# Filter stage of a Mamba, attention and spectral-filter block: the lower left quarter of the block Toeplitz product with three products in place of four

## The chip, the cores and the metric

One core of one Trainium2 chip runs the whole program. The metric is device time in microseconds from one launch; lower is better. TensorE does the matrix products, VectorE (DVE) and ScalarE (ACT) the elementwise work, GpSimd (POOL) a share of it, and SyncE (SP) issues the DMAs. All data is float32. The matmuls of this stage read their operands as pairs of a rounded part ("high", in a float32r tile) and a rest ("low").

## The reference, cut to what matters

The program computes a two-way Mamba block with group norm, then causal attention, then a mixture of four spectral filter experts, on 4 batches of 1024 tokens with 64 channels. The change touches only the last part and the preparation of its filters:

```python
def _stu_conv(phi, u, n):            # phi (L, 16), u (b, sl, 64)
    Vf = rfft(phi, n=n, axis=0)
    Uf_p = rfft(u, n=n, axis=1); Uf_m = rfft(u * sgn3, n=n, axis=1)
    U_plus  = irfft(Vf[None, :, :, None] * Uf_p[:, :, None, :], n=n, axis=1)[:, :sl]
    U_minus = irfft(Vf[None, :, :, None] * Uf_m[:, :, None, :], n=n, axis=1)[:, :sl] * sgn
    return U_plus, U_minus
out = einsum('btkd,k,kde->bte', U_plus, s, Mpp) + einsum('btkd,k,kde->bte', U_minus, s, Mpm)
# x = t + stu mixture (experts see the first 1/1, 1/2, 1/4, 1/8 of the tokens) + 3 taps of u
```

In the time domain each of the 16 filters is a causal convolution of 1024 tokens, that is, a product with a lower triangular Toeplitz matrix. Even and odd tokens are held apart, so each filter gives two sources (even, odd) and two lags.

## The kernel before, in words

The program has three stages with a barrier between them: the Mamba stage, the attention stage and the filter stage (`expert_stage`), which begins 667 us into the profile.

In the filter stage the batches are taken in two pairs (`q`), the 64 channels of both batches of a pair side by side on 128 rows. For each pair there are 16 filters, so 32 filters in all. A filter has two steps, `source` 0 and 1. A step is one call of `convolve`: for a Toeplitz product of 512 half-rate tokens in blocks of 128, it multiplies token blocks (stationary operand, `u_high` or `u_low`) with shifted windows of the filter (`hankel`, moving operand), two lags at a time. The out bank of 512 columns for the first half of the tokens needs block offsets 0 and 1, the one for the second half offsets 0 to 3. Each offset takes three matmuls (`TERMS`: high by high, low by high, high by low): 18 matmuls a step, of which 12 have 512 columns and 6 have 256.

TensorE's order for a filter is: step 0, then `mix` of the filter before (10 matmuls with `block_mix`), then step 1. The first filter of each pair of batches is followed by `taps_and_residual`. ScalarE copies each half out of PSUM into a float32r tile (L1973), one copy for each batch of the pair, 64 rows each; VectorE subtracts that copy from the PSUM value and writes the low part (L2010). Each source has its own PSUM tile `ps_conv` of two banks, so TensorE waits only for the low parts of two steps before. SyncE loads the filter windows of filter m (`load_hankel`, L1607) once filter m-2 is done, into one of two slots. GpSimd forms `block_mix` for the coming filter (L1733, L1737).

The filters' rows are made in the attention stage: GpSimd reverses and splits `phi` (`filter_rows`, L1637 and L1638), SyncE stores them in DRAM (L1618) and loads the first two windows; GpSimd goes on with `weigh_and_sum`, `even_matrices` (L1697, which overwrites the memory in which `phi` lay) and then `rstd2`, a step of the attention chain (L1055).

The work of each engine is written out by hand in program order; counting semaphores tie the engines together.

Of the kernel before, what the change touches and what calls it, by code (L numbers as in the profile page):

```python
# [26 lines left out]
B = 4  # L27
# [20 lines left out]
PADS = 640  # L48
BLOCKS = 2
# [53 lines left out]
def norm_tensors(nc, ctx):  # L103
# [6 lines left out]
    g.mixed = sb("mixed", [C, L])  # L110
# [27 lines left out]
def load_sums(sp, g, b):  # L138
# [69 lines left out]
def mamba_stage(nc, ins, a, g, e, x1):  # L208
# [4 lines left out]


    with ExitStack() as ctx:
# [105 lines left out]
        with nc.Block() as block:  # L321

            @block.sync
            def _(sp):
# [52 lines left out]
                def unit(u, i):  # L377
                    sp.wait_ge(bc_out, 16 * (u + 1))
                    for s in range(N):
# [6 lines left out]
                        if i == 0 and u:  # L386
                            if s == 9:
                                store_sums(sp, g, u // 2 - 1)
                            if s == 11:
                                load_sums(sp, g, u // 2 - 1)  # L390
# [579 lines left out]
def attention_stage(nc, ins, a, g, e, x1, x2, u_all, u_high, u_low):  # L970

    with ExitStack() as ctx:
# [66 lines left out]
        with nc.Block() as block:  # L1039

            @block.sync
            def _(sp):
                store_sums(sp, g, B - 1)
                load_sums(sp, g, B - 1)
# [3 lines left out]
            def _(pool):  # L1048
# [24 lines left out]
                weigh_and_sum(nc, pool, e, EXPERTS + 2, 2 * EXPERTS)  # L1073
                even_matrices(nc, pool, e)
# [486 lines left out]
def weight_tensors(nc, ctx):  # L1561

    def sb(name, shape, dt=F32):
# [10 lines left out]
        ar_step ar_ready block_step block_ready passed phi_in plus_in minus_in"""  # L1574
    (e.logits_in, e.weights_in, e.w_step, e.softmax_ready, e.wk_ready, e.sum_step, e.rows_step, e.rows_ready,
     e.filters_out, e.ar_step, e.ar_ready, e.block_step, e.block_ready, e.passed, e.phi_in, e.plus_in,
     e.minus_in,
# [5 lines left out]
def expert_tensors(nc, ctx, e):  # L1583
# [19 lines left out]
    e.filters = nc.dram_tensor("filters", (FILTERS, 4, PADS), F32, kind="Internal").ap()  # L1603


def load_hankel(sp, e, k, slot):
    sp.dma_start(e.hankel[slot][:, :, 0:H + 1].bitcast(F32),  # L1607
                 bass.AP(e.filters.tensor, k * 4 * PADS, [[1, 128], [PADS, 4], [1, H + 1]])
                 ).then_inc(e.hankel_in[slot], 16)


def load_expert_weights(sp, ins, e):
# [8 lines left out]
    for slot in range(2):  # L1621
        load_hankel(sp, e, slot, slot)

# [7 lines left out]
def filter_rows(nc, pool, e):  # L1631
# [3 lines left out]
    for lag in range(2):  # L1635
# [3 lines left out]
            e.rows[:, 2 * lag + 1, 0:H], reverse, e.rows[:, 2 * lag, 0:H].bitcast(F32), ALU.subtract))  # L1639

# [51 lines left out]
def even_matrices(nc, pool, e):  # L1692

    pool.wait_ge(e.filters_out, 16)
# [45 lines left out]
def expert_stage(nc, ins, att, e, x2, u_all, u_high, u_low, out):  # L1740
# [11 lines left out]
    with ExitStack() as ctx:  # L1752
# [12 lines left out]
        shifted = sb("shifted", [C, BANKS, H])  # L1765
# [6 lines left out]
        ps_conv = [ctx.enter_context(nc.psum_tensor(f"ps_conv{i}", [128, 2, 2, H // 2], F32)) for i in range(2)]  # L1772
# [7 lines left out]
        names = """pads_ready ut_psum ut_high ut_low conv_half conv_psum conv_high conv_low mixed_in shift_ready  # L1780
            out_done"""
        (pads_ready, ut_psum, ut_high, ut_low, conv_half, conv_psum, conv_high, conv_low, mixed_in, shift_ready,
# [10 lines left out]
        with nc.Block() as block:  # L1793

            @block.sync
            def _(sp):
                for q in range(PAIRS):
                    with sp.Fori(1 - q, FILTERS // 2) as pair:
                        for slot in range(2):
                            k = 2 * pair + slot  # L1800
                            sp.wait_ge(conv_psum, STEPS * (q * FILTERS + k - 1))
                            load_hankel(sp, e, k, slot)
                for q in range(PAIRS):
# [22 lines left out]
            def _(pe):  # L1826
# [7 lines left out]
                def convolve(slot, q, source):  # L1834

                    shift = source
                    hankel = e.hankel[slot]
# [241 lines left out]
```

## Time and profile before

| what | value |
| --- | --- |
| median of 3 runs | 981.84 us (980.28 to 983.69) |
| the profiled execution's own time | 984.49 us |
| its span, first to last instruction | 982.6 us |
| busy over the span | PE 86%, PEld 50%, DVE 74%, ACT 52%, POOL 54% |
| mean granted TensorE clock | 0.939 of full speed |

PE stands for matmuls, PEld for the loads of the stationary operand. In a timeline row the first number is the start in microseconds from the span's start, the second the time covered, "x2" means that two instructions are merged in the row, and the bracket at the end tells how long the engine sat idle before it and what ended that. All durations that the prediction uses come from this one execution.

### The profile page before, as it was taken

To read this page: it belongs to the slowest core of one execution; us is meant where nothing else is said; L and a number is where in the kernel's file an instruction comes from. 1 tells how busy PE (TensorE), PEld (TensorE's weight loads), DVE (VectorE), ACT (ScalarE), POOL (GpSimd) and SP (SyncE) were. 2 spreads that over 40 slices of the span, in tenths; PEclk is the share of its full clock that TensorE was granted. 3 is DMA by queue.
4 is the path that set the end of the run, shared out by engine and by line. 5 is a ranking of instruction groups with operands and counts; after the bars stand their busy time and mean duration, and the time that the engine had idled before them with its cause. 6 is when DMAs were issued, how large, how long until landed. Compare 5 with 4: busy or idle time off the path is not lost. (4 is left out here: it accounts for less than half of the span.)

```text
span 982.6 us, 10220 instructions
## 1 busy us (share of the span) xinstructions
PE 841.4 (86%) x3004; PEld 493.4 (50%) x3004; DVE 722.8 (74%) x774; ACT 511.6 (52%) x706; POOL 534.3 (54%) x366
## 2 busy tenths in 40 slices
PE   5768798887989788886586998958999999999996
PEld 1223233332333233332234554527888888888885
DVE  1999989989999999999965446634666566565664
ACT  4635656555566556644305366545455555454553
POOL 4577878879888897876625965311222221122220
PEclk9779989899999999997977899988999999999998
DMA  7778897878979898787609900001243344233432
GB/s 174 275 241 336 300 311 254 324 265 277 334 235 371 276 322 286 299 308 233 219 0 103 180 1 1 1 0 44 87 128 114 100 128 128 87 99 115 128 108 63
DMA packets 75348, 178.23 MB, mean 181 GB/s; under 512 B 24514, under 2 KB 25044, under 8 KB 75300
## 3 DMA queue, kind: packets, MB, share of 16 engines
q1 hardware_dynamic: 75316, 177.85, 56.8%
q8 instruction: 14, 0.23, 0.1%
q14 instruction: 18, 0.15, 0.0%
HBM read 175.57 MB, written 2.26 MB: 181 GB/s over the span
## 5 line engine op out<-in xcount | busy, mean ns | idle before, releaser
L451 POOL TENSOR_TENSOR prod<-hidden,c_wide 128x1024 f32<-128x1024 f32 x128 | 300.8, 2356 | 99.0 <-DVE hidden L882 93.4
L546 PE MATMUL ps_y<-prod,ident 128*128 128x512 f32 x512 | 247.3, 627 | 42.8 <-POOL prod L451 42.7
L882 DVE TENSOR_TENSOR_SCAN hidden<-decay,ps_d 128x1024 f32<-128x1024 f32 x99 | 226.0, 2283 | 9.9
L1850 PE MATMUL ps_conv<-hankel,u_high 128*128 128x512 f32 (+1 forms) x768 | 215.5, 362 | 0.0
L546 PEld LDWEIGHTS ps_y<-prod,ident 128*128 128x128 f32 x512 | 98.2, 198 | 185.7 <-issue 117.1
L1850 PEld LDWEIGHTS ps_conv<-hankel,u_high 128*128 128x128 f32 x768 | 138.7, 189 | 25.4 <-issue 0.3
L2010 DVE TENSOR_TENSOR stack<-ps_conv,stack 64x512 fp32r<-64x512 f32 x128 | 88.3, 690 | 68.8 <-ACT stack L1973 66.4
L1850 PE MATMUL ps_conv<-hankel,u_low 128*128 128x512 f32 (+1 forms) x384 | 138.1, 360 | 0.0
L1733 POOL CAST block_mix<-even 128x256 fp32r (+1 forms) x32 | 12.7, 398 | 218.9 <-PE ps_tail L1832 218.9
L868 DVE TENSOR_TENSOR ps_d<-ps_x,b_wide 128x1024 f32<-128x1024 f32 x99 | 122.0, 1232 | 4.5
L2010 DVE TENSOR_TENSOR qk<-ps_conv,qk 64x512 fp32r<-64x512 f32 x128 | 88.3, 690 | 50.0 <-ACT qk L1973 47.2
L1973 ACT ACTIVATE stack<-ps_conv 64x512 fp32r<-64x512 f32 x128 | 76.0, 594 | 82.3 <-PE ps_conv L1850 80.4
L1973 ACT ACTIVATE qk<-ps_conv 64x512 fp32r<-64x512 f32 x128 | 76.0, 594 | 62.3 <-PE ps_conv L1850 60.3
L732 ACT ACTIVATE decay<-dt_b,a_neg_b 128x1024 f32<-128x1024 f32 x51 | 58.0, 1144 | 70.8 <-DVE hidden L882 70.4
L1850 PEld LDWEIGHTS ps_conv<-hankel,u_low 128*128 128x128 f32 x384 | 72.9, 190 | 13.8
L732 ACT ACTIVATE decay<-dt_f,a_neg_f 128x1024 f32<-128x1024 f32 x48 | 54.2, 1142 | 38.4 <-DVE hidden L882 37.1
L441 POOL TENSOR_TENSOR drive<-dtx,b_wide 128x1024 f32<-128x1024 f32 x29 | 68.4, 2358 | 6.7 <-ACT dtx L727 6.7
L1460 DVE TENSOR_REDUCE max_parts<-ps_s 128x1 f32<-128x512 f32 (+1 forms) x48 | 27.5, 598 | 27.1 <-PE ps_s L1144 13.4
L882 DVE TENSOR_TENSOR_SCAN hidden<-ps_d,drive 128x1024 f32<-128x1024 f32 x14 | 32.1, 2290 | 9.3 <-ACT ps_d L738 5.4
L1055 POOL TENSOR_TENSOR small<-small,minus_half 128x8 f32<-128x8 f32 x4 | 6.6, 1645 | 57.3 <-DVE small L1430 57.3
L1324 ACT ACTIVATE probs<-ps_t 128x512 f32<-128x512 f32 (+1 forms) x48 | 24.8, 521 | 23.0 <-PE ps_o L1186 22.8
L882 DVE TENSOR_TENSOR_SCAN hidden<-ps_w,drive 128x1024 f32<-128x1024 f32 x15 | 34.2, 2279 | 0.0
(306 smaller groups left out, 1187.7 us busy)
## 6 DMA issues: line engine op xcount, KB each, us to landing
b_wide<-bc_rows SPq DMA_DIRECT2D x128, 512.0 KB, 5.5
c_wide<-bc_rows SPq DMA_DIRECT2D x128, 512.0 KB, 5.4
hankel<-filters SPq DMA_DIRECT2D x32, 1026.0 KB, 5.2
plus<-in_M_phi_plus SPq DMA_DIRECT2D x2, 1024.0 KB, 13.2
minus<-in_M_phi_minus SPq DMA_DIRECT2D x2, 1024.0 KB, 18.8
x_pair<-in_x SPq DMA_DIRECT2D x2, 768.0 KB, 8.6
bc_rows<-dt_low SPq DMA_DIRECT2D x8, 128.0 KB, 4.9
out<-plus SPq DMA_DIRECT2D x4, 256.0 KB, 4.9
```

Source lines behind the costliest of these rows:

```text
L441: nc.gpsimd.tensor_tensor(drive[:, :], dtx[:, :], b_wide[s % BC_DEEP][:, :], ALU.mult).then_inc(share_ready, 1)
L451: nc.gpsimd.tensor_tensor(prod[k % PAIR][:, :], hidden[k % DEEP][:, :], c_wide[s % BC_DEEP][:, :], ALU.mult).then_inc(prod_ready, 1)
L546: mm = nc.tensor.matmul(out, ident[:, :], halves(prod[k % PAIR])[h], start=False, stop=(k % N == N - 1))
L732: nc.scalar.activation(decay[decay_slot(s, last)][:, :], dt[i][:, :], ACT.Exp, scale=a_neg[i][:, s:s + 1]).then_inc(decay_ready, 1)
L868: nc.vector.tensor_tensor(ps_d[:, :], ps_x[:, :], b_wide[s % BC_DEEP][:, :], ALU.mult).then_inc(drive_ready, 1)
L882: nc.vector.tensor_tensor_scan(hidden[k % DEEP][:, order], left[:, order], right[:, order], 0.0, ALU.mult, ALU.add).then_inc(hidden_ready, 1)
L1324: nc.scalar.activation(probs[n % 2][:, 0:hi - lo], ps_t[n % 2][:, 0:hi - lo], ACT.Exp).then_inc(probs_ready, 1)
L1460: nc.vector.tensor_reduce(max_parts[:, i, at // H:at // H + 1], ps_s[c % 2][:, 0:n], AX.X, ALU.max, negate=True).then_inc(part_ready, 1)
L1733: nc.gpsimd.tensor_copy(dst[:, :, 0, :], src).then_inc(e.block_step, 1)
L1850: mm = nc.tensor.matmul(out, pairs[q][wp][:, 2 * delta + source, :], rows, start=(delta == 0 and term == 0), stop=(delta == 2 * half + 1 a ...
L1973: nc.scalar.activation(stacks[slot][0:C, source, b, :, half * 2 * HEAD:(half + 1) * 2 * HEAD], ps_conv[source][lanes(b), half, :, :], ACT. ...
L2010: nc.vector.tensor_tensor(low, ps_conv[source][lanes(b), half, :, :], high.bitcast(F32), ALU.subtract).then_inc(conv_low, 1)
```

## The change

The second half of the out tokens takes from the first half of the in tokens a 2 by 2 block of Toeplitz blocks (offsets 1, 2, 2 and 3 in units of 128). Its four block products are replaced by three: one of the filter windows at offset 2 with the difference of the two token blocks (`gap`), which both outputs share with opposite sign, and one for each output with the sum of two filter windows (`hankel_sums`). The shared product lands in a PSUM tile of its own (`ps_common`, both sources in one bank), ScalarE keeps it as two copies with signs +1 and -1 in SBUF (`common`), and VectorE adds it to the late half (`late`). The late half's high and low parts are then made from that SBUF tile. The early half has one PSUM bank for both sources (`ps_early`), where before each source had its own.

The sums of filter rows are made by GpSimd between `weigh_and_sum` and `even_matrices`, stored by SyncE, and loaded with each filter beside the windows. `gap` and its two parts are made by VectorE as the stage's first work. Some tiles move: `shifted` lies in the memory of `x1`, `gap_parts` in `k_low`, `common` and `late` in attention tiles.

```diff
+def load_sums(sp, e, hankel_sums, k, slot):
+    sp.dma_start(hankel_sums[slot][:, :, 0:SUM_ROW - 1].bitcast(F32),
+                 bass.AP(e.filter_sums.tensor, k * 4 * SUM_TAPS, [[1, 128], [SUM_TAPS, 4], [1, SUM_ROW - 1]])
+                 ).then_inc(e.hankel_in[slot], 16)
...
+def filter_sums(nc, pool, e):            # called between weigh_and_sum and even_matrices
+    pool.wait_ge(e.filters_out, 16)
+    for lag in range(2):
+        reverse = e.phi[:, lag::2][:, ::-1]
+        chain_on(pool, e.sums_ready, 3 * lag + 1, nc.gpsimd.tensor_tensor(
+            e.pair_sum, reverse[:, 128:128 + SUM_TAPS], reverse[:, 0:SUM_TAPS], ALU.add))
+        chain_on(pool, e.sums_ready, 3 * lag + 2, nc.gpsimd.tensor_copy(e.sum_rows[:, 2 * lag, :], e.pair_sum))
+        chain_on(pool, e.sums_ready, 3 * lag + 3, nc.gpsimd.tensor_tensor(
+            e.sum_rows[:, 2 * lag + 1, :], e.pair_sum, e.sum_rows[:, 2 * lag, :].bitcast(F32), ALU.subtract))
...
 def even_matrices(nc, pool, e):
-    pool.wait_ge(e.filters_out, 16)
+    pool.wait_ge(e.sums_out, 16)
...
 # SyncE: at the end of load_expert_weights
+    sp.wait_ge(e.sums_ready, 6)
+    sp.dma_start(e.filter_sums..., e.sum_rows...).then_inc(e.sums_out, 16)
 # SyncE: filter stage
+                for slot in range(2):
+                    load_sums(sp, e, hankel_sums, slot, slot)
...
                             load_hankel(sp, e, k, slot)
+                            load_sums(sp, e, hankel_sums, k, slot)
 # TensorE (terms issues the three matmuls of TERMS with n columns for each lag)
-                    for half in range(2):
-                        for delta in range(2 * half + 2):
...
+                    at_least(pe, common_kept, 2 * t)
+                    terms(ps_common[source], gaps[q], source, hankel, row, H - 1 - 2 * HEAD, HEAD, source,
+                          first=True, last=True).then_inc(common_psum, 1)
+                    at_least(pe, early_low, 2 * t)
+                    terms(ps_early, data, source, hankel, row, H - 1, 2 * HEAD, source, first=True)
+                    terms(ps_early[:, :, HEAD:], data, 2 + source, hankel, row, H - 1, HEAD, source,
+                          last=True).then_inc(conv_early, 1)
+                    at_least(pe, late_ready, t - 1)
+                    terms(late_out, data, 4 + source, hankel, row, H - 1, 2 * HEAD, source, first=True)
+                    terms(late_out[:, :, HEAD:], data, 6 + source, hankel, row, H - 1, HEAD, source)
+                    terms(late_out[:, :, 0:HEAD], data, 2 + source, sums, SUM_ROW, 2 * HEAD - 1, HEAD, source)
+                    terms(late_out[:, :, HEAD:], data, source, sums, SUM_ROW, HEAD - 1, HEAD, source,
+                          last=True).then_inc(conv_psum, 1)
...
-                    pe.wait_ge(e.hankel_in[slot], 16 * (q * FILTERS // 2 + pair + 1))
-                    at_least(pe, conv_low, PIECES * (t - 1))
+                    pe.wait_ge(e.hankel_in[slot], 32 * (q * FILTERS // 2 + pair + 1))
+                    if first and q == 0:
+                        pe.wait_ge(gap_ready, 3)
 # ScalarE, each step
-                        for half in range(2):
-                            act.wait_ge((conv_half, conv_psum)[half], t + 1)
-                            for b in range(2):
-                                nc.scalar.activation(stacks[slot][0:C, source, b, :, half * 2 * HEAD:(half + 1) * 2 * HEAD],
-                                                     ps_conv[source][lanes(b), half, :, :], ACT.Copy).then_inc(conv_high, 1)
+                        act.wait_ge(common_psum, t + 1)
+                        at_least(act, late_ready, t - 1)
+                        for block, sign in enumerate((1.0, -1.0)):
+                            nc.scalar.activation(common[source][:, :, block, :], ps_common[source], ACT.Copy,
+                                                 scale=sign).then_inc(common_kept, 1)
+                        act.wait_ge(conv_early, t + 1)
+                        for b in range(2):
+                            nc.scalar.activation(stacks[slot][0:C, source, b, :, 0:2 * HEAD], ps_early[lanes(b), :, :],
+                                                 ACT.Copy).then_inc(early_high, 1)
+                        act.wait_ge(late_ready, t + 1)
+                        for b in range(2):
+                            nc.scalar.activation(stacks[slot][0:C, source, b, :, 2 * HEAD:],
+                                                 late[source][lanes(b), :, :, :].rearrange("p l k i -> p l (k i)"),
+                                                 ACT.Copy).then_inc(late_high, 1)
 # VectorE, each step (before: four subtractions from ps_conv, each after its copy)
+                        for b in range(2):
+                            dve.wait_ge(early_high, 2 * t + b + 1)
+                            nc.vector.tensor_tensor(low, ps_early[lanes(b), :, :], high.bitcast(F32),
+                                                    ALU.subtract).then_inc(early_low, 1)
+                        dve.wait_ge(conv_psum, t + 1)
+                        dve.wait_ge(common_kept, 2 * t + 2)
+                        at_least(dve, late_low, 2 * (t - 1))
+                        nc.vector.tensor_tensor(late[source]..., ps_late[source],
+                                                common[source]..., ALU.add).then_inc(late_ready, 1)
+                        for b in range(2):
+                            dve.wait_ge(late_high, 2 * t + b + 1)
+                            nc.vector.tensor_tensor(low, late[source][lanes(b), :, :, :]...,
+                                                    high.bitcast(F32), ALU.subtract).then_inc(late_low, 1)
 # VectorE, start of the stage: gap = difference of token blocks, its high part, its low part
```

## Rows read from the trace of the kernel before

**Rows 1.** Chain that ended last, two filters: start, time covered, engine, tile, line.
```profile
851.25 7.13 PE ps_conv L1850 x36
858.38 0.48 PE ps_low L1832 x4
858.86 0.47 PE ps_mid L1832 x2
...
860.25 7.12 PE ps_conv L1850 x36
```

**Rows 2.** Busy time by stretch: us, then PE, PEld, DVE, ACT, POOL, clock, DMA share, GB/s.
```profile
851.25:860.25 9.00, 9.00 (x47) 7.60 (x47) 5.52 (x9) 4.75 (x8) 2.17 (x4) 1.00 0.37 118
...
560.00:600.00 40.00, 36.64 (x174) 21.14 (x173) 24.45 (x65) 20.37 (x45) 26.62 (x13) 1.00 0.11 38
...
973.70:976.50 2.80, 2.67 (x10) 1.73 (x10) 1.34 (x4) 1.68 (x4) 0.00 (x0) 0.76 0.00 0
```

**Rows 3.** Groups of instructions from 600 us on, by form: busy us, mean ns, idle before.
```profile
L1850 PE MATMUL ps_conv<-hankel,u_high 128*128 128x512 f32 x512 | 184.2, 400 | 0.0
...
L2010 DVE TENSOR_TENSOR stack<-ps_conv,stack 64x512 fp32r<-64x512 f32 x128 | 88.3, 690 | 68.8 <-ACT stack L1973 66.4
L1973 ACT ACTIVATE stack<-ps_conv 64x512 fp32r<-64x512 f32 x128 | 76.0, 594 | 82.3 <-PE ps_conv L1850 80.4
```

**Rows 4.** Timeline of one step's half on ScalarE and VectorE.
```profile
800.14 1.21 ACT L1973 ACTIVATE stack<-ps_conv 64x512 fp32r<-64x512 f32 x2 [1.73 <-PE ps_conv L1850]
800.76 1.41 DVE L2010 TENSOR_TENSOR stack<-ps_conv,stack 64x512 fp32r<-64x512 f32 x2 [1.53 <-ACT stack L1973]
```

**Rows 5.** Timeline of ScalarE in the attention stage: copies from PSUM and from SBUF.
```profile
568.59 0.39 ACT L1324 ACTIVATE probs<-ps_t 128x256 f32<-128x256 f32 x1
568.87 1.06 ACT L1295 ACTIVATE xn_t<-ps_p 64x512 f32<-64x512 f32 x2
...
654.32 0.63 ACT L1289 ACTIVATE u_high<-u_all 128x512 fp32r<-128x512 f32 x1
654.86 0.37 ACT L1324 ACTIVATE probs<-ps_t 128x256 f32<-128x256 f32 x1
```

**Rows 6.** Timeline of the start of the filter stage.
```profile
667.56 1.08 PE L1909 MATMUL ps_low<-ident,u_all 128*128 128x128 f32 x4 [9.30 <-PEq L1039]
670.85 0.70 PE L1850 MATMUL ps_conv<-hankel,u_high 128*128 128x512 f32 x1
678.30 0.33 PE L1832 MATMUL ps_low<-u_t,ar_mix 128*128 128x128 f32 x2
685.51 0.50 PE L1850 MATMUL ps_conv<-hankel,u_high 128*128 128x512 f32 x1
675.92 4.29 DVE L2010 TENSOR_TENSOR qk<-ps_conv,qk 64x512 fp32r<-64x512 f32 x6
```

**Rows 7.** Landing of L1607's loads, of L1618's store; packets in one 9 us stretch.
```profile
DMA to landing us min/median/max: 5.1/5.2/8.3
...
DMA to landing us min/median/max: 3.6/3.6/3.6
...
DMA packets 528, 1.05 MB, mean 117 GB/s; under 512 B 16, under 2 KB 16, under 8 KB 528
```

**Rows 8.** Timeline: last mix of the program; then where the first pair's result is taken.
```profile
973.78 0.74 PE L1832 MATMUL ps_low<-stack,block_mix 128*128 128x256 f32 x4 [2.13 <-DVE stack L2010]
...
827.43 1.27 DVE L2016 TENSOR_TENSOR plus<-ps_tail,shifted 64x512 f32<-64x512 f32 x2
829.40 0.34 PE L1832 MATMUL ps_low<-u_t,ar_mix 128*128 128x128 f32 x2
```

**Rows 9.** GpSimd: `filter_rows`, then `even_matrices` and what follows it.
```profile
L1638 POOL TENSOR_TENSOR even<-even x2: 1348/1348/1348, 529.6 to 531.8; 16x512 fp32r<-16x512 f32 x2
...
572.30 9.68 POOL L1697 TENSOR_TENSOR even<-plus,minus 128x1024 f32<-128x1024 f32 x4 [0.17 <-POOL minus L1685]
594.55 1.65 POOL L1055 TENSOR_TENSOR small<-small,minus_half 128x8 f32<-128x8 f32 x1 [12.57 <-DVE small L1430]
```

More of the change, by code:

```diff
@@ L48 @@
 PADS = 640
+SUM_TAPS = 384
+SUM_ROW = 258
 BLOCKS = 2
@@ L208, in mamba_stage @@
 def mamba_stage(nc, ins, a, g, e, x1):
+    a.x1, a.both = x1, g.both
     with ExitStack() as ctx:
@@ L1832, in add_out @@
                     return nc.tensor.matmul(dst, w_block, data, start=first, stop=True, skip_group_check=True)
-                def convolve(slot, q, source):
-                    shift = source
-                    hankel = e.hankel[slot]
-                    row = H + 2
-                    for half in range(2):
-                        for delta in range(2 * half + 2):
-                            first = 128 * delta
-                            lo = max(first, half * 2 * HEAD)
-                            n = (half + 1) * 2 * HEAD - lo
-                            out = ps_conv[source][:, half, :, 2 * HEAD - n:]
-                            for term, (wp, dp) in enumerate(TERMS):
-                                rows = bass.AP(hankel, dp * row + H - 1 + first - lo,
-                                               [[4 * row, 128], [2 * row + shift, 2], [-1, n]])
-                                mm = nc.tensor.matmul(out, pairs[q][wp][:, 2 * delta + source, :], rows,
-                                                      start=(delta == 0 and term == 0),
-                                                      stop=(delta == 2 * half + 1 and term == len(TERMS) - 1))
-                        mm.then_inc((conv_half, conv_psum)[half], 1)
@@ new lines, in _, with terms @@
+                gaps = [[part[:, :, 2 * q:2 * q + 2, :].rearrange("p s b c -> p s (b c)") for part in gap_parts]
+                        for q in range(PAIRS)]
+                def terms(out, data, tile, rows, pitch, at, n, shift, first=False, last=False):
+                    for term, (wp, dp) in enumerate(TERMS):
+                        mm = nc.tensor.matmul(out, data[wp][:, tile, :],
+                                              bass.AP(rows, dp * pitch + at, [[4 * pitch, 128], [2 * pitch + shift, 2], [-1, n]]),
+                                              start=first and term == 0, stop=last and term == len(TERMS) - 1)
+                    return mm
@@ new lines, in convolve @@
+                def convolve(slot, q, source, t):
+                    hankel, sums, data = e.hankel[slot], hankel_sums[slot], pairs[q]
+                    row = H + 2
+                    late_out = ps_late[source]
+                    at_least(pe, common_kept, 2 * t)
[11 more added lines that the diff above has]
+                          last=True).then_inc(conv_psum, 1)
```

62 lines of the change are left out of this document (41 added, 21 removed).

## Prediction

> **What bounds the kernel now.** I read the chain of waits first. In the filter stage it is TensorE and nothing else [rows 1]: 36 convolution matmuls in 7.12 us, 10 mix matmuls in 1.87 us (858.38 to 860.25), 9.0 us for a filter, with no wait between. The busy times of the same 9 us say the same: PE 9.00, VectorE 5.52, ScalarE 4.75 [rows 2]. The groups by form show where the slack lies: the copies L1973 waited 82 us for TensorE and the subtractions L2010 69 us for the copies [rows 3]. So a shorter TensorE program pays here for as long as ScalarE and VectorE keep up, and the question is what their new order does.
>
> **TensorE's work.** The mean of a matmul (400 ns for 512 columns, [rows 3]) is latency, since they overlap. Spacing counts: ps_mid has 2 of 512 columns in 0.47 us, 0.235 each; ps_low has 4 of 256 in 0.48, 0.12 each [rows 1]. Check: 24 x 0.235 + 12 x 0.12 = 7.08, against 7.12 measured. Before, a step has 12 and 6. After, it has 6 of 512 (early 3, late 3) and 15 of 256 (common 3, early 3, late 9): 3 more instructions, but 768 columns fewer. For a filter that is 12 x 0.235 + 30 x 0.12 = 6.4 us, 0.7 less. With the mix, 8.27 in place of 9.0. The other bound, that a matmul of 256 columns costs more in runs of 9 than in runs of 4, is not borne out by [rows 1]; at 0.13 it would cost 0.3 a filter.
>
> **The new loop between ScalarE and VectorE.** Before, a step's four copies and four subtractions ran behind TensorE with no way back in a step. Now a step t has, on ScalarE in this order: two copies of the common product, C; two early copies, E; then a wait for VectorE's addition; two late copies, L. On VectorE: two early subtractions, the addition, two late subtractions. Both are strictly in order. So L(t) is followed by C(t+1) and E(t+1); the last E(t+1) releases the second early subtraction; behind that stands the addition of t+1; and it releases L(t+1). This ring closes once a step, without TensorE in it. Nothing in it overlaps but the first subtraction with the second E. Its length, from the start of E:
> - first E to first subtraction: 800.14 to 800.76, 0.62 [rows 4]
> - two subtractions 1.41 [rows 4]; the second starts after 0.71, later than the second E ends plus hand-over, so it adds nothing
> - addition, 128x512 with one operand in PSUM: the trace has no such form; the subtraction with one operand in PSUM takes 0.69 [rows 3], plus 0.03 ahead of it (1.41 less two times 0.69) and 0.03 hand-over (0.62 less 0.594): 0.75
> - two L, source in SBUF: the nearest row is 0.63 [rows 5], not the 0.594 of PSUM. In the pair of [rows 4] the second starts 0.02 after the first ends (1.21 less 2 x 0.594), so 2 x 0.65 = 1.30. Other pairs overlap: u_high takes 0.63 but the next starts after 0.54, and the xn_t pair takes 1.06 for two of 0.58 [rows 5]. The two L read different halves of the rows, like the pair L1973; I take 1.30, lower bound 1.08
> - two C, 128x256 from PSUM: 0.38 by itself, the next starting 0.28 later (568.59 to 568.87) [rows 5]. They read the same rows, so I take 0.28 each, 0.56; upper bound 2 x 0.40 = 0.80
>
> Sum 0.62 + 1.41 + 0.75 + 1.30 + 0.56 = 4.64 us a step, bounds 4.42 and 4.88. A filter is two: 9.28, bounds 8.84 and 9.76. TensorE needs 8.27 and must now wait, 1.0 us a filter, where it starts the early product and needs the early bank free (`early_low`; one bank where each source had its own). Against 9.0 now (8.98 over the stage) this is +0.30 a filter, bounds -0.14 and +0.78.
>
> ScalarE's busy time is 0.56 + 1.21 + 1.30 = 3.1 a step, VectorE's five times 0.69 with gaps 3.55: neither is full. It is the order that binds. Break-even is a ring of 4.49 a step; under 4.13 TensorE binds again.
>
> On ScalarE the trace shows both: the pair L1973 does not overlap, the xn_t pair does, by 0.1 us. The Trainium skill ("ScalarE: Activation LUTs", section "What ACT_TABLE_LOAD costs") states that back-to-back ACTIVATEs overlap by about 93 ns, without exception. By that rule the L pair would be 1.11 and E 1.09. The ring would be some 0.2 shorter, which is rival A; the 1.21 of L1973 speaks against the rule for pairs that change rows, and the sum goes by that row.
>
> **Filters outside the steady state.** By following the same durations through: the two filters after each taps block find ScalarE and VectorE caught up (the block is 7.2 us of TensorE alone, 678.30 to 685.51, [rows 6]) and run at TensorE's pace, -0.7 each. That is three in all, -2.1, since of the second pair's two one is used up: there ScalarE's four `shift` copies now stand behind L, so VectorE's fold ends about 2.2 us after the convolution, where before it ended 0.7 ahead of the taps (828.70 against 829.40) [rows 8]; +2.2 less the 0.7 is +1.5. The remaining 27 filters at +0.30: +8.1.
>
> **Start of the stage.** TensorE began its first convolution at 670.85 [rows 6]. It now waits for 32 on the load semaphore, so for the first sums, issued when the stage begins (about 667.9). A load of 1,026 KB takes 5.2 us to landing, up to 8.3 for the two issued together [rows 7]; of it 3.3 are transfer (DMA share 0.37 of 9 us, [rows 2]). Half the bytes in as many packets: 3.5 if bytes count, 5.2 if packets count, 8.3 at worst. I take 4.8: landed at 672.5, 1.7 late. Then step 0 (3.2) and common 0.36 end at 676.1, but the early product of step 1 waits for the early subtractions of step 0. VectorE is busy with `u_t` until 675.9 [rows 6], then does them to 677.4. So both steps end at 677.5 + 1.07 + 1.78 = 680.35, against 678.30 [rows 6]: **+2.05** (bounds +1 and +5.5). The three `gap` instructions on VectorE (3 x 0.69) end at 669.7, when `u_t` was waiting for ScalarE anyway: nothing.
>
> **Tail.** The last mix waited 2.13 us for the low parts [rows 8]. Now the addition (0.75) stands ahead, and L is 0.04 slower: +0.8.
>
> **What lies beside other work.** The GpSimd sums: 6 instructions of 16x384, from 1.35 us for 16x512 [rows 9] at most 6 us with waits, then SyncE's store (the like store took 3.6, [rows 7]): `even_matrices` is about 9.6 us later. It ended at 582.0 and GpSimd then waited 12.6 us for VectorE [rows 9], so 3 us of cover are left; were it 10 us longer, 7 would fall on the attention chain. Filter loads: windows plus sums take 7.5 (by bytes) to 9.2 us (by packets) from the release, with a second issue on SyncE; the time until they are needed is one filter, 9.3, plus the 1.0 of TensorE's wait. Hidden, but nearly used up. The windows' slots and `mixed_in` are as before.
>
> **Sum.** +8.1 -2.1 +1.5 +2.05 +0.8 = +10.3. For the unseen waits (each addition now has three) I add up to 1 us in all: **+11** on the profiled execution's 984.49. The median shown is 2.65 less, 981.84; the forecast is 993.
>
> **Rivals.**
> A. All copies overlap by 0.1 us. For it: most pairs in the attention stage do [rows 5]. Against: the 256 copies of L1973 do not. Ring 4.40, a filter 8.8, 27 x -0.18 = -4.9, with the other terms -3: 979. By the Trainium skill's rule above this is the case.
> B. The other side: the ring does not bind and TensorE does. This needs a ring under 4.13, for instance if the sequencers let L or the addition start on data ready earlier, or VectorE's forms with both rows full were faster than 0.69. Then 31 x -0.72 = -22, start and tail +3: 962. Decides below 4.49 a step. Against it: each link is a row, and their sum would have to be 0.5 off.
> C. The ring is longer: C without overlap (0.80), hand-overs double, or DMA or GpSimd slows VectorE. Ring 4.88, 27 x 0.78 = 21, plus 2.3: 1005.
> D. TensorE's waits of 1 us lower its clock. In the attention stage it was idle 8% of the time at a clock of 1.00 [rows 2]; after the 2.1 us idle of the tail it was 0.76 over 2.8 us [rows 2, 8]. If it were at 1.2 GHz for a tenth of the stage, 30 us of work would cost 26 more, of which the waits hide 3: 1015.
>
> **How the numbers follow.** Forecast 0.58, A 0.17, B 0.08, C 0.14, D 0.03. What can be told from no change here is about 0.3%, 3 us. Faster: B and half of A, 0.16. Same: the other half, and a little of the forecast's low end: 0.10. Slower: 0.74. The forecast's own range is 987 to 999; the range of 8 in 10 is 978 to 1007.
>
> **What would show it.** In the steady stretch, a filter of 9.3 us with TensorE 8.3 busy; the idle time ahead of the first early matmul, ended by VectorE's early subtraction, about 1 us once a filter; ScalarE's L released by the addition with no slack, and the addition starting 0.03 after the second subtraction. Clock 1.00. If TensorE waits on the load semaphore instead, the load budget was wrong; if it waits nowhere, B holds. If `rstd2` at 594.55 moves, the cover on GpSimd was not there.

## The result, and the profile after

| | before | after |
|---|---|---|
| median (range), us | 981.09 (980.28 to 983.69), 4 runs | 996.58 (993.78 to 1001.44), 4 runs |
| ratio | | 1.0159 [1.0114, 1.0203] |
| profiled execution, us (span) | 984.49 (982.6) | 996.15 (994.4) |
| filter stage in the profile, first transpose to end | 315.0 | 330.8 |
| from one mix to the next, most filters | 8.97 to 9.00 | 9.32 to 9.35 |

Slower by 15.5 us in the medians, 1.6%; 993 was forecast, with 987 to 999 as its own range and 978 to 1007 as that of 8 in 10. The profiled executions differ by 11.7 only, since the stage began at 663.59 in the one and at 667.56 in the other: the work ahead of it, which the change doesn't touch there, took a few us less in that execution (over all profiles of this study the stage began between 658 and 668). Below, the stage is compared, +15.8 us, which fits the medians.

The share of the chain of waits, after; TensorE, which held all of [rows 1], is hardly there:
```profile
DVE 14%; ACT 8%; issue 6%; PE 4%; DVEq 1%; ACTq 0%
DVE mixed_wide L2081 4%; DVE qk L2086 3%; DVE stack L2086 2%; DVE qk L2076 2%; DVE stack L2076 2%; ACT late L2026 2%; ACT stack L2034 2%; ACT qk L2034 2%; PE ps_conv L1881 1%; PE ps_tail L1873 1%; ACT stack L2030 1%; ACT qk L2030 1%; PE ps_low L1873 1%; PE ps_mid L1873 1%; ACT u_t L2012 0%
```
Busy time by stretch, after, columns as in [rows 2]: one filter and 120 us of the steady stretch, step 1 at the start, and the last mix.
```profile
860.00:869.30 9.30, 8.61 (x52) 7.56 (x52) 7.28 (x11) 5.97 (x12) 2.98 (x4) 1.00 0.56 172
...
700.00:820.00 120.00, 110.51 (x671) 97.03 (x670) 94.39 (x130) 77.00 (x156) 38.86 (x50) 1.00 0.54 170
...
675.00:678.00 3.00, 3.00 (x15) 2.71 (x13) 2.53 (x4) 2.14 (x5) 0.00 (x0) 0.55 0.00 0
...
984.80:987.60 2.80, 2.77 (x9) 2.41 (x10) 0.81 (x2) 1.19 (x2) 0.00 (x0) 0.52 0.00 0
```
No engine is full: of 9.30 us TensorE has 8.61, VectorE 7.28, ScalarE 5.97. What binds is in the timelines. ScalarE, two steps of the steady stretch (L2034 is the late copies L, L2026 the common ones C, L2030 the early ones E):
```profile
802.02 1.29 ACT L2034 ACTIVATE stack<-mixed_wide 64x512 fp32r<-64x512 f32 x2 [1.58 <-DVE mixed_wide L2081]
803.33 0.66 ACT L2026 ACTIVATE late<-ps_conv 128x256 f32<-128x256 f32 x2
803.88 1.21 ACT L2030 ACTIVATE stack<-ps_conv 64x512 fp32r<-64x512 f32 x2
806.71 1.28 ACT L2034 ACTIVATE stack<-mixed_wide 64x512 fp32r<-64x512 f32 x2 [1.63 <-DVE mixed_wide L2081]
```
VectorE in the same us (L2086 late subtractions, L2076 early ones, L2081 the addition):
```profile
802.68 1.83 DVE L2086 TENSOR_TENSOR stack<-mixed_wide,stack 64x512 fp32r<-64x512 f32 x2 [0.70 <-ACT stack L2034]
804.54 1.41 DVE L2076 TENSOR_TENSOR stack<-ps_conv,stack 64x512 fp32r<-64x512 f32 x2
805.98 0.69 DVE L2081 TENSOR_TENSOR mixed_wide<-ps_conv,late 128x512 f32<-128x512 f32 x1
807.38 1.40 DVE L2086 TENSOR_TENSOR stack<-mixed_wide,stack 64x512 fp32r<-64x512 f32 x2 [0.70 <-ACT stack L2034]
```
L, C, E without a gap on ScalarE; 0.66 after the first E the early subtractions; 0.03 behind them the addition; 0.04 behind that the next L. From L to L 4.69 us, and 4.64 to the one after (it starts at 811.35). TensorE waits for the early subtractions once a filter (its waits from 700 to 820 us, 12.9 filters: total, times, longest):
```profile
PE ps_conv L1881 <- DVE qk L2076: 5.2, 7, 0.7
PE ps_conv L1881 <- DVE stack L2076: 4.3, 6, 0.7
```
The start of the stage and the last mix, TensorE, after [rows 6, 8]:
```profile
663.59 1.09 PE L1959 MATMUL ps_low<-ident,u_all 128*128 128x128 f32 x4 [9.29 <-PEq L1044]
667.86 0.62 PE L1881 MATMUL ps_conv<-hankel,k_low 128*128 128x256 f32 x3 [0.62 <-DMA hankel_sums<-filter_sums]
673.42 0.50 PE L1881 MATMUL ps_conv<-hankel,u_high 128*128 128x512 f32 x1 [1.56 <-DVE qk L2076]
677.90 0.34 PE L1873 MATMUL ps_low<-u_t,ar_mix 128*128 128x128 f32 x2
...
984.83 1.13 PE L1873 MATMUL ps_low<-stack,block_mix 128*128 128x256 f32 x4 [3.88 <-issue]
```

### The profile page after: what moved, and what is told of

Same layout as the page of the kernel before. It is cut to its first block and busy times, and to the rows that moved or that the text cites. A ratio compares the mean times of both kernels' runs of the same rounds, so it can differ in the third digit from the quotient of the medians.

```text
span 994.4 us, 11024 instructions
## 1 busy us (share of the span) xinstructions
PE 830.2 (83%) x3196; PEld 493.4 (50%) x3196; DVE 780.2 (78%) x841; ACT 551.3 (55%) x834; POOL 566.5 (57%) x372
## 5 line engine op out<-in xcount | busy, mean ns | idle before, releaser
L1881 PE MATMUL ps_conv<-hankel,u_high 128*128 128x512 f32 (+1 forms) x512 | 142.4, 350 | 21.3 <-DVE qk L2076 11.9
L1881 PEld LDWEIGHTS ps_conv<-hankel,u_high 128*128 128x128 f32 x512 | 92.9, 190 | 39.7 <-DVE qk L2076 15.0
L1881 PE MATMUL ps_conv<-hankel,u_low 128*128 128x512 f32 (+1 forms) x256 | 87.8, 343 | 0.0
L2034 ACT ACTIVATE qk<-mixed_wide 64x512 fp32r<-64x512 f32 x64 | 40.4, 631 | 53.0 <-DVE mixed_wide L2081 52.2
L2034 ACT ACTIVATE stack<-mixed_wide 64x512 fp32r<-64x512 f32 x64 | 40.4, 631 | 52.0 <-DVE mixed_wide L2081 51.2
L2086 DVE TENSOR_TENSOR qk<-mixed_wide,qk 64x512 fp32r<-64x512 f32 x64 | 50.3, 786 | 23.3 <-ACT qk L2034 22.3
L2086 DVE TENSOR_TENSOR stack<-mixed_wide,stack 64x512 fp32r<-64x512 f32 x64 | 49.6, 774 | 23.3 <-ACT stack L2034 22.3
L2076 DVE TENSOR_TENSOR stack<-ps_conv,stack 64x512 fp32r<-64x512 f32 x64 | 44.1, 689 | 21.2 <-ACT stack L2030 19.8
L1881 PE MATMUL ps_conv<-hankel_sums,u_high 128*128 128x256 f32 x256 | 57.2, 286 | 0.0
L2076 DVE TENSOR_TENSOR qk<-ps_conv,qk 64x512 fp32r<-64x512 f32 x64 | 44.1, 689 | 8.0 <-ACT qk L2030 6.5
L2026 ACT ACTIVATE late<-ps_conv 128x256 f32<-128x256 f32 x128 | 42.2, 382 | 11.9 <-PE ps_conv L1881 5.7
```

The lines of the kernel that those rows point to most:

```text
L1881: mm = nc.tensor.matmul(out, data[wp][:, tile, :], bass.AP(rows, dp * pitch + at, [[4 * pitch, 128], [2 * pitch + shift, 2], [-1, n]]), st ...
L2026: nc.scalar.activation(common[source][:, :, block, :], ps_common[source], ACT.Copy, scale=sign).then_inc(common_kept, 1)
L2034: nc.scalar.activation(stacks[slot][0:C, source, b, :, 2 * HEAD:], late[source][lanes(b), :, :, :].rearrange("p l k i -> p l (k i)"), ACT. ...
L2076: nc.vector.tensor_tensor(low, ps_early[lanes(b), :, :], high.bitcast(F32), ALU.subtract).then_inc(early_low, 1)
L2086: nc.vector.tensor_tensor(low, late[source][lanes(b), :, :, :].rearrange("p l k i -> p l (k i)"), high.bitcast(F32), ALU.subtract).then_in ...
```

## The experiments

"us a filter" is the distance from one mix to the next in the steady stretch, "stage" as in the table. R is the prediction's loop: L, C, E on ScalarE, then subtractions and addition on VectorE. Each median stands against runs of the kernel before on the same chip (980.8 to 982.0). Measured, in one place:

| run | us (ratio, 95%) | us a filter | stage |
|---|---|---|---|
| changed kernel | 996.58 (1.0159 [1.0114, 1.0203]) | 9.33 | 330.8 |
| e1_one_common_copy | 991.41 (1.0102 [1.0070, 1.0133]) | 9.13 | 323.0 |
| e2_two_early_banks | 996.43 (1.0133 [1.0061, 1.0205]) | 9.33 | 331.4 |
| e3_old_pe_load | 998.91 (1.0163 [1.0101, 1.0224]) | 9.33 | 331.0 |
| e4_common_copies_moved | 990.53 (1.0099 [1.0064, 1.0134]) | 9.15 | 324.0 |
| e5_sums_loaded_once | 997.26 (1.0171 [1.0130, 1.0212]) | 9.33 | 331.0 |
| e6_late_in_psum | 983.81 (1.0022 [0.9990, 1.0055]) | 8.93 | 317.8 |
| e7_little_gpsimd | 987.46 (1.0077 [1.0046, 1.0108]) | 9.11 | 325.0 |
| e8_psum_and_taps_later | 984.26 (1.0037 [1.0007, 1.0066]) | 8.93 | 319.1 |
| e9_common_behind_early_psum | 973.93 (0.9925 [0.9901, 0.9950]) | 8.58 | 309.0 |
| e12_common_behind_early | 976.84 (0.9956 [0.9925, 0.9986]) | 8.6 to 8.9 | 311.3 |
| e10_ut_split_in_two | 972.92 (0.9905 [0.9882, 0.9928]) | 8.58 | 305.3 |
| e13_one_copy_little_gpsimd | 976.07 (0.9958 [0.9930, 0.9987]) | 8.74 | 311.0 |

**First, four that take one suspect each: a copy in the loop, the bank that TensorE waits for, TensorE's saving, the order on ScalarE.**

e1: the negated copy is left out, so half of the addition's operand is stale. (In all code cuts below, lines that only follow from the ones shown are left out.)
```
- for block, sign in enumerate((1.0, -1.0)):
+ for block, sign in ((0, 1.0),):
- dve.wait_ge(common_kept, 2 * t + 2)          # TensorE's wait: 2 * t -> t
+ dve.wait_ge(common_kept, t + 1)
```


> The changed kernel with only the first of ScalarE's two copies of the common product; the second half of the tile `common` keeps old values, so the late half of the outputs is not the reference's. Theory R (a ring between ScalarE and VectorE, without TensorE in it, sets the pace): a second copy costs 0.28 us of the ring, twice a filter, so a filter takes 8.77 us in place of 9.33; over 29 filters -16 us against the changed kernel (996.6), near 980. Rival P (TensorE and its one early bank set the pace): no instruction of TensorE changes, a filter stays at 9.33 and the time within 2 us of 996.6.

It moved, in R's direction, by a third of R's 0.56. VectorE's timeline shows why:
```profile
802.26 1.96 DVE L2086 TENSOR_TENSOR stack<-mixed_wide,stack 64x512 fp32r<-64x512 f32 x2 [0.70 <-ACT stack L2034]
804.25 1.41 DVE L2076 TENSOR_TENSOR stack<-ps_conv,stack 64x512 fp32r<-64x512 f32 x2
805.69 0.69 DVE L2081 TENSOR_TENSOR mixed_wide<-ps_conv,late 128x512 f32<-128x512 f32 x1
807.08 1.40 DVE L2086 TENSOR_TENSOR stack<-mixed_wide,stack 64x512 fp32r<-64x512 f32 x2 [0.70 <-ACT stack L2034]
```
VectorE now runs without a gap but for the first L: 0.70 + late subtractions + 1.44 + 0.72. That is a second ring, V: 4.26 a step with a late pair of 1.40, 4.82 with the 1.96 that the pair takes once a filter (802.26 to 807.08). Two steps make 9.1. The 1.96 falls beside GpSimd's `block_mix` subtraction (e13 tests that).

e2: an early bank for each source; `ps_mid` moves onto `ps_low`'s bank, so that two products of the mix are summed in one bank. Since the new bank takes part in the transposes at the start, TensorE also waits there for all of `u_t` ahead of step 1, and ScalarE's `shift` copies wait for the whole last mix.
```
- at_least(pe, early_low, 2 * t)
+ at_least(pe, early_low, 2 * (t - 1))
- terms(ps_early, ...)          + terms(ps_early[source], ...)
```


> The changed kernel with a PSUM bank of its own for the early product of each source; the bank is taken from ps_mid, whose sums are added into ps_low instead, so part of the output is not the reference's. The wait of TensorE on the early subtractions (the only wait that the profile shows in the steady stretch, about 0.8 us a filter) goes. Rival P (the early bank that both sources share is the cost): a filter falls from 9.33 to TensorE's own 8.3 us, -29 us, near 967. Theory R: the wait only moves to another place of TensorE's program, the filter stays at 9.33, and the time within 3 us of 996.6.

The same 9.33. The wait only moved, to ahead of the mix; it is TensorE's one wait left from 700 to 820:
```profile
PE ps_low L1875 <- issue: 9.2, 12, 0.8
```
So the early bank, where TensorE is seen to wait, is where the ring's lateness shows and not what costs. (The steady stretch is what counts here; the two added waits lie at the start and between the pairs of batches.)

e3: the three common matmuls are issued twice, into the same bank.
```
+ terms(ps_common[source], gaps[q], source, hankel, ..., first=True, last=True)
```


> The changed kernel with the three matmuls of the common product issued twice in every step: 6 more matmuls of 256 columns a filter, 0.72 us, which is just what the change had saved on TensorE. The result is the same. Theory R: TensorE has 1.0 us a filter to spare, so a filter stays at 9.33 to 9.40 us and the time within 3 us of 996.6; the saving on TensorE was worth nothing here. Rival P: +0.72 us a filter, 10.05, +21 us, near 1018.

TensorE's saving is given back, and nothing moves (9.33):
```profile
700.00:820.00 120.00, 119.92 (x747) 106.40 (x746) 94.05 (x129) 76.40 (x154) 39.47 (x52) 1.00 0.56 170
```

e4: on ScalarE, C of the even step ahead of the last filter's odd L, C of the odd step behind its E.
```
+ keep_common(t, 0); keep_late(t - 1, 1, 1 - slot)
+ keep_early(t, 0, slot); keep_late(t, 0, slot)
+ keep_early(t + 1, 1, slot); keep_common(t + 1, 1)
```


> The changed kernel with another order on ScalarE alone: the copies of the common product are taken out from between the late copies and the early copies, into the time in which ScalarE waits for VectorE's addition (for source 0 ahead of the late copies of the step before, for source 1 behind the early copies). Theory R: the ring loses 0.56 us a step, from 4.66 to 4.10, less than TensorE's 4.13, so TensorE sets the pace again at 8.3 to 8.5 us a filter: -24 to -30 us, 967 to 973, faster than the kernel before the change (981). Rival P: 9.33 as before, 996.6.

A miss by over 0.6 us a filter, though better than the changed kernel. What is late instead? The next four asked that: GpSimd beside VectorE, the operand in SBUF, the transfers, the taps.

**Then: what holds the new order back.**

e7: e4, with GpSimd's copy and subtraction for `block_mix` cut to 2 of 64 columns, so the mix uses stale weights.
```
- nc.gpsimd.tensor_tensor(dst[:, :, 1, :], src, ...)
+ nc.gpsimd.tensor_tensor(dst[:, :, 1, 0:2], src[:, :, 0:2], ...)     # tensor_copy likewise
```


> e4 with GpSimd's four instructions a filter for block_mix cut to 2 of 64 columns each (the mix then uses old values, so the outputs are not the reference's). The late subtractions still have both operands in SBUF. Theory G: no collision, all subtractions at 0.69 us, a filter of 8.3 to 8.6 us, 967 to 974. Rival Q: 9.0 to 9.15, as e4.

9.11 against 9.15: taking the collision away doesn't free e4; something else is as late.

e6: e4, with the addition made in place in PSUM.
```
- tensor_tensor(late[source], ps_late[source], common[source], ALU.add)
+ tensor_tensor(ps_late[source], ps_late[source], common[source], ALU.add)
- at_least(pe, late_ready, t - 1)      + at_least(pe, late_low, 2 * (t - 1))
```


> e4 with the sum of the late half written back into its PSUM bank in place of SBUF, so that the late copies and the late subtractions read PSUM again; TensorE waits for the late subtractions of two steps before. e4 took 9.15 us a filter where the ring alone would have allowed 8.3. Theory G: what is left is a collision of VectorE's late subtractions, which since the change have both operands in SBUF, with GpSimd's preparation of block_mix (a subtraction that lies beside it takes 1.1 us in place of 0.69, and the early subtraction behind it starts 0.6 us late). With an operand in PSUM they take 0.69 at all times, as before the change: a filter of 8.3 to 8.5 us, -20 to -24 us against e4 (990.5), 967 to 971. Rival Q: the order of waits alone holds e4 at 9.15 (the early bank, freed once a step); the late half's place changes ScalarE by 0.04 a copy only: 9.0 to 9.15, 987 to 990.

8.93, still far from the 8.3 to 8.5. Both timelines show a loop that e4's order itself had made, here in e6, ScalarE and TensorE (L2020 is C):
```profile
809.03 0.66 ACT L2020 ACTIVATE late<-ps_conv 128x256 f32<-128x256 f32 x2
810.49 0.66 ACT L2020 ACTIVATE late<-ps_conv 128x256 f32<-128x256 f32 x2 [0.80 <-PE ps_conv L1881]
```
```profile
809.29 0.28 PE L1881 MATMUL ps_conv<-hankel_sums,u_high 128*128 128x256 f32 x1
809.75 0.63 PE L1881 MATMUL ps_conv<-hankel,k_low 128*128 128x256 f32 x3 [0.18 <-ACT late L2020]
```
TensorE's last matmul of a step starts at 809.29, so at about 809.41 it wants the common bank, which both sources share; C of the odd step, now at the end of ScalarE's queue, ends at 809.69. TensorE makes the next common product at 809.75, and C of the even step, with the late copies queued behind it, waits 0.80 for it. I call it S.

e8: e6 with the taps one filter later.


> e6 with the block of taps and residual moved one filter later, behind the first step of the second filter of each pair of batches, so that it no longer waits for the fold of the pair before. The result is the same. In the changed kernel the interval around the second block was 18.1 us where 16.3 stood before the change and 15.6 would be TensorE's own. Expected: 2 to 3 us less than e6, 965 to 968; if the fold is not what TensorE waited for, the same as e6.

No gain: 8.93, stage 319.1 against 317.8. The expectation fell. The wait for the fold is gone (1.47 us in e6), but TensorE now waits 1.99 at nearly the same place, for ScalarE's C, which stands behind the four `shift` copies:
```profile
828.74 0.60 PE L1881 MATMUL ps_conv<-hankel,k_low 128*128 128x256 f32 x3 [1.99 <-ACT late L2020]
```

e5: the changed kernel, the sums loaded only once a slot, so later filters use the first sums.
```
- load_sums(sp, e, hankel_sums, k, slot)      # in the loop; TensorE's count on the load semaphore to match
```


> The changed kernel without the loads of the filters' window sums inside the filter loops: only the first two are loaded, so from the third filter on the sums are those of another filter and the outputs are not the reference's. 30 loads of 514 KB go. Theory R (the ring between ScalarE and VectorE) and theory G (below) both expect nothing: a filter stays at 9.33 us and the time within 3 us of the changed kernel's 996.6, since each load had landed 6.6 us after its issue with 9.3 to spare. A rival, that the added transfers slow the stage (DMA share 0.56 in place of 0.37), expects a filter nearer 9.0, -10 us.

```profile
700.00:820.00 120.00, 110.49 (x667) 96.77 (x667) 93.79 (x130) 76.35 (x155) 38.19 (x52) 1.00 0.37 114
```
The DMA share is back at the 0.37 of [rows 2], the time is the changed kernel's. The added transfers cost nothing there.

**Last: the order that S and R both ask for, and the loop by itself.**

e9: common behind early on TensorE and on ScalarE, so C falls into ScalarE's wait for the addition; the addition in PSUM.
```
# TensorE: terms(ps_early ...), then terms(ps_common ...), then late
# ScalarE: E; C; wait late_ready; L
```


> The changed kernel with the late sum in PSUM (as e6) and another order: TensorE issues the common product behind the early one in each step, ScalarE copies early, common, late. Theory G (collision with GpSimd) has fallen with e7, which stayed at 9.11 us a filter. Theory S, from the trace of e6 (8.93 a filter): the ring of ScalarE and VectorE no longer binds there, but the two sources share the bank of the common product, and its copies for source 1, moved behind the early copies, end 1.9 us after the early product, 0.3 later than TensorE wants the bank back. With the common product behind the early one its bank is wanted again a full step later, and its copies lie in ScalarE's wait for the addition: ring 4.05 a step, TensorE's 4.13 to 4.2 binds: 8.3 to 8.5 us a filter, 29 x -0.5 = -15 us against e6 (983.8), 966 to 972. Rival: the single early bank binds, 8.9 as e6.

By its busy time TensorE binds again, with 119.64 of 120 us, at 8.58 a filter where 8.27 was worked out and 8.3 to 8.5 expected. Most of the 0.31 lies between two steps: the odd step's first matmul starts 0.27 behind the last one and the next 0.35 behind it, where 0.12 and 0.235 are usual.
```profile
700.00:820.00 120.00, 119.64 (x727) 105.44 (x726) 96.32 (x140) 84.66 (x169) 29.77 (x56) 1.00 0.59 184
```
```profile
804.04 0.28 PE L1881 MATMUL ps_conv<-hankel_sums,u_high 128*128 128x256 f32 x1
804.31 0.50 PE L1881 MATMUL ps_conv<-hankel,u_high 128*128 128x512 f32 x1
...
802.85 1.41 DVE L2076 TENSOR_TENSOR qk<-ps_conv,qk 64x512 fp32r<-64x512 f32 x2
804.36 0.70 DVE L2081 TENSOR_TENSOR ps_conv<-ps_conv,late 128x512 f32<-128x512 f32 x1
```
That matmul needs the early bank, and VectorE's early subtractions end at 804.26, 0.05 ahead of it. The changed kernel shows the same at its recorded wait: subtractions to 805.95, matmul at 806.01, the next 0.34 later. So a wait of about 0.15 for VectorE is left, which the idle time doesn't show because the ends of matmuls are modelled. VectorE's own round is 4.24 a step here (addition at 804.36, the next at 808.60), 8.48 a filter, more than the 8.27 of TensorE; the ring of 4.05 in the expectation left it out. This is read from the traces and not tried by a run.


e12: the same order with the addition in SBUF, as the change has it.


> As e9, but the late sum stays in SBUF as in the changed kernel; so it differs from the changed kernel by the order of work alone. Late copies cost 0.04 us more each, and the late subtractions lie open to GpSimd (0.8 to 1.1 us in place of 0.69 when it works). Theory S: 8.4 to 8.9 us a filter, 970 to 983. If order alone does not do it (theory P), 9.1 to 9.3, 990 to 996.

The stage is 2.3 us longer than e9's and 19.5 shorter than the changed kernel's: the order is nearly all of it.

e10: e9, with each engine's work on the second half of `u_t` put behind its first step.
```
+ take_ut(0)    ...    if fresh and source == 0: take_ut(1)      # ScalarE
+ split_ut(0)   ...    if fresh and source == 0: split_ut(1)     # VectorE
```


> As e9, with the eight pieces of u_t at the start of the stage taken in two parts of four, the second behind ScalarE's and VectorE's early work of the first step. In the changed kernel TensorE waited 1.56 us for the early subtractions of the first step, and its granted clock then lay at 0.55 for 3 us. Without that wait: 2 to 4 us less than e9, 963 to 969, the same steady filters. If the clock falls for another reason, at most 1.5 us less.

The stage is 3.7 us shorter than e9's, as expected, though the median is not at 963 to 969: that was counted from e9's expected 966 to 972, and e9 took 973.93. The start in e9, then in e10:
```profile
670.00:674.00 4.00, 2.14 (x7) 1.85 (x8) 3.22 (x6) 2.00 (x5) 0.00 (x0) 0.72 0.00 0
```
```profile
670.00:674.00 4.00, 3.20 (x20) 2.92 (x21) 3.13 (x5) 2.74 (x7) 1.98 (x4) 1.00 0.30 100
```
This version, with all that the change computes, is faster than both kernels, than the one before by a little under 1%: 972.92 us, 0.9905 [0.9882, 0.9928] of before. Against e9's 973.93 the medians alone don't separate it; the stage in the profiles does.

e13: e1 and e7's cut together, on the changed kernel's order.


> e1 (one copy of the common product) with GpSimd's four instructions a filter cut to 2 of 64 columns each; two things are left out, so the outputs are not the reference's. e1 took 9.13 us a filter where the ring gave 8.77. Theory V: in e1 a second ring, on VectorE alone but for one copy (late subtractions, early subtractions, addition, first late copy), took over: 0.70 + 1.40 + 1.44 + 0.72 = 4.26 us, but 4.82 in the step in which GpSimd stretches the late pair to 1.96: 9.09 a filter. Without GpSimd's work it is 8.5 and the first ring binds at 8.77: 8.75 to 8.85 a filter. If the collision is not the reason, 9.1 as e1.

```profile
804.57 1.29 ACT L2034 ACTIVATE qk<-mixed_wide 64x512 fp32r<-64x512 f32 x2 [1.58 <-DVE mixed_wide L2081]
...
808.95 1.28 ACT L2034 ACTIVATE stack<-mixed_wide 64x512 fp32r<-64x512 f32 x2 [1.58 <-DVE mixed_wide L2081]
```
4.38 from L to L: the ring of 4.64 less one C of 0.28 is 4.36. With GpSimd out of the way the ring R has the length that was worked out for it, and e1's missing 0.4 a filter was the collision.

## Why the prediction was right, and where its terms were off

**The mechanism.** Right: a ring through two in-order queues, without TensorE. Its links as worked out and as measured: E to subtraction 0.62 (0.66 and 0.61 in turn), subtractions 1.41 (1.41), addition with its hand-overs 0.75 (0.76), two L 1.30 (1.31), two C 0.56 (0.55). The sum was 4.64, the measured steps are 4.69 and 4.64 (L at 802.02, 806.71 and 811.35). The longer one is VectorE's: its late pair, stretched to 1.83 beside GpSimd, ends at 804.51, and the early subtractions start at 804.54 without idle time, so the collision already costs 0.05 a filter here. e13 takes one link away and gets its length back; e3 gives TensorE its old load back and loses nothing; e2 and e5 rule out the bank and the transfers. The wait forecast at about 1 us once a filter, ahead of an early matmul, is there with 0.73 (9.5 us in 13 waits); TensorE's busy time is the longer for it, 8.61 where 8.27 was worked out. Part of that is wait too: by the spacing the matmul of 806.01 could have come at 805.14 (the three from 804.78 at 0.12 each), 0.87 before it did.

**ScalarE's pairs.** C reads the same rows twice: 128x256 took 0.38 and the second began after 0.28, so they overlap by 0.1. L and E take other rows the second time: 1.29 for two of 0.63, 1.21 for two of 0.594, no overlap. The Trainium skill ("ScalarE: Activation LUTs", section "What ACT_TABLE_LOAD costs") says that back-to-back ACTIVATEs overlap by about 93 ns, as measured on tiles of 128 rows; the trace agrees for C, which has 128 rows, and not for the 64-row pairs L and E. This decided the sign of the steady term: by the rule the ring is 4.4 and the kernel is slightly faster. (By that estimate the L pair would be 1.17, two of 0.63 less 0.093, and not the prediction's 1.11; rival A's 4.40 stands, since L and C would overlap too.)

A change of rows alone doesn't decide it. C (all rows) and the first E (rows 0 to 63) overlap by 0.11 (803.33 + 0.66 against 803.88), and in e12 the second L (rows 64 to 127, from SBUF) and the first E (rows 0 to 63, from PSUM) by 0.09 (806.49 + 1.28 against 807.68), while here the second L and the first C don't (802.02 + 1.29 against 803.33). All of these fit one reading: an instruction overlaps the one before it where it starts at the same row as ScalarE's last read from the same memory, SBUF or PSUM. No run tried this by itself.

**Term by term,** against the stage's +15.8:
- 27 filters at +0.30, +8.1: measured 9.33 against 8.99, 27 x 0.34 = +9.2. Right.
- three filters at TensorE's pace, -0.7 each: the first after either taps block took 8.57, -0.4 each, -0.8 for the two; the one at the start is in the next term.
- the start, +2.05 less one 0.7, so +1.35: from the first transpose to the first mix 24.83 against 21.60, **+3.2**. The first sums landed 4.3 us after their issue, where 4.8 was taken (667.9 + 4.8 is 672.7, not the prediction's 672.5): TensorE began 0.98 later after its first transpose than before, with 0.62 of it shown as a wait, less than the 1.7 feared, and that for the early subtractions 1.56, about as worked out. But behind it the clock was 0.55 (675 to 678), so that step 1's matmuls of 256 columns came 0.21 apart in place of 0.12. I had priced the wait and left out what it does to the clock, though rival D and [rows 8] had it.
- second taps, +1.5: the interval took 18.12 against 16.3, +1.8. Right, and in its cause too: TensorE waits 2.25 for the fold, where 2.2 was worked out. But e8 shows that the fold is not the only thing late there.
```profile
835.16 0.42 PE L1873 MATMUL ps_low<-u_t,ar_mix 128*128 128x128 f32 x2 [2.25 <-DVE plus L2092]
```
- the tail, +0.8: **about +2.2**. The wait ahead of the last mix is 3.88 against 2.13, and the clock over it 0.52 against 0.76 [rows 2]. The wait is longer by more than the addition (1.75 against 0.75), since the ring's backlog stands ahead of it: the last addition starts at 981.93, right behind the early subtractions, when TensorE's last product had been done since about 980.9.

Measured, these make 15.6. The forecast's 10.3 lacked 1.9 at the start and 1.4 at the tail, 1.1 in the 27 filters and 0.9 around the taps. That the clock behind a wait is most of the first I take from the spacing, and e10, which removes that wait, gives back 3.7 against e9; the tail was not tried by itself. That the profiled executions differ by 11.7, near the forecast's +11, is in part luck: the untouched work ahead of the stage was shorter in the second.

**What lay beside.** GpSimd's sums were hidden as forecast, with the cover nearly used up: 2.78 us left where 12.57 were [rows 9], 3 were worked out.
```profile
577.79 10.00 POOL L1727 TENSOR_TENSOR even<-plus,minus 128x1024 f32<-128x1024 f32 x4 [2.40 <-issue]
590.57 1.65 POOL L1060 TENSOR_TENSOR small<-small,minus_half 128x8 f32<-128x8 f32 x1 [2.78 <-DVE small L1436]
```
The sums landed in the median 6.6 us after issue, the windows in 5.7, and were waited for only at the start. The slack that the prediction read from [rows 3] is that of one of the two tiles; with the other (62.3 and 50.0 us) the copies waited 145 us and the subtractions 119, which makes its point stronger.

**The rivals.** B and A fell with the 9.33. C (a longer ring) had its causes half right: GpSimd does slow VectorE, but in the changed kernel all but 0.05 a filter of this falls where ScalarE is not through yet, and only e1 laid it bare. D came true in two short stretches and nowhere in the steady one.

## What to carry to other kernels

When two in-order engines hand work back and forth within a step, add up the links of that ring before crediting a saving on the engine that binds now; here 0.7 us a filter saved on TensorE became 0.34 lost, and e3 shows that the saving had no value at all. Look in such a ring for an instruction that could stand where its engine waits (here two copies, by the order alone worth the whole loss and more), and then ask which bank the new order frees later. A wait at the seam of a stage is also to be priced at the clock behind it.

## What the runs showed of the hardware that was not expected

**Two SBUF operands beside GpSimd.** VectorE's late subtractions in the changed kernel, and GpSimd's subtraction, first there, then in e6, where the same subtraction has its first operand in PSUM (busy us, mean ns | idle before):
```profile
L2086 DVE TENSOR_TENSOR qk<-mixed_wide,qk 64x512 fp32r<-64x512 f32 x64 | 50.3, 786 | 23.3 <-ACT qk L2034 22.3
...
L1767 POOL TENSOR_TENSOR block_mix<-minus,block_mix 128x256 fp32r<-128x256 f32 x32 | 36.0, 1126 | 0.0
```
```profile
L2098 DVE TENSOR_TENSOR qk<-ps_conv,qk 64x512 fp32r<-64x512 f32 x64 | 44.1, 689 | 40.9 <-ACT qk L2032 39.9
...
L1767 POOL TENSOR_TENSOR block_mix<-minus,block_mix 128x256 fp32r<-128x256 f32 x32 | 23.5, 735 | 0.0
```
Where the two meet, one of 0.69 takes up to 1.12, and GpSimd's 0.73 becomes 1.13; with a PSUM operand both are flat. In e7, with two SBUF operands as here and GpSimd's instructions cut to 2 columns, no late subtraction takes over 0.75, so it is GpSimd beside it that costs. The Trainium skill ("Perfetto Trace Analysis", section "Optimizing Scalar/DVE Operations") says that GpSimd and VectorE share a read port of SBUF. The traces agree, with these numbers as the price.

**Pairs and rows.** VectorE's pairs too have 0.03 us between them where the rows change, as ScalarE's L and E have 0.02 to 0.03; the fold's additions, which all start at the same row, begin 0.61 apart for 0.68 each (832.54 and 833.15).

**The clock after short waits.** At the seam of the stage, after VectorE and ScalarE had been waited for, the clock was 0.55, near the lower of the two levels (1.2 of 2.4 GHz), over the 3 us from 675; in e9, with a wait of 2.08 that ends at 671.86, it was 0.72 from 670 to 674 and 0.90 from 674 to 680; in e10, with no such wait, 1.00 in both. In the steady stretch of the changed kernel a wait of 0.7 once a filter left it at 1.00. What tells these apart beyond the length of the wait and the idle time ahead of the stage was not tried.
